# A linear-attention and routed-block kernel on one core: output projections and units moved among the head steps, some rotation sums given to GpSimd, two more banks at the start

## The chip, the cores and the metric

The kernel runs on one core of one Trainium2 chip. The time is device microseconds of one execution. The engines are TensorE (PE), VectorE (DVE), ScalarE (ACT), GpSimd (POOL) and SyncE (SP), which issues nearly all transfers. Each engine runs its own list of instructions in order and waits on semaphores.

## What is computed

```python
xn = layernorm(x)                                   # x: 2048 x 512, fp32
out = x + attn(xn) + ffn(xn)

def attn(x):                                        # 16 heads of width 32, blocks with decay
    q, k, v, u = split(x @ W_qkvu.T)
    q, k = silu(q), silu(k)
    o = decayed_linear_attention(q, k, v)           # a state per head is carried over the tokens
    o = o * rsqrt(mean(o * o) + 1e-6)
    return (u * o) @ W_out.T

def ffn(hidden):                                    # 256 of the 2048 tokens, chosen by w_router
    sel = hidden[top_256(hidden @ w_router)]
    h = rms_norm(sel, ln1)
    q, k, v = rope(h @ wq + bq), rope(h @ wk + bk), h @ wv + bv   # 16 heads of 128, 8 of k and v
    x1 = sel + softmax_causal(q @ k.T / sqrt(128)) @ v @ wo
    mlp = silu(rms_norm(x1, ln2) @ w_gate) * (rms_norm(x1, ln2) @ w_up) @ w_down
    return hidden with the rows of sel replaced by g * (x1 + mlp) + (1 - g) * sel   # g = sigmoid(score)
```

## The kernel before

Nearly every fp32 matmul is made of three in the type fp32r: an operand is split into a rounded high part (made by ACT) and the remainder, the low part (made by DVE or GpSimd), and PE adds high x high, high x low and low x high in one bank (`split_matmuls`, L1177).

**Start.** SP loads s_head, s_hid, x(0), x(1) and the four quarters of K's weights (L383 to L388). ACT makes decay tables from s_head (`decay_tables`, L516), then the highs of the weights and of xT. DVE norms the first two tiles (`ln_stats`, `ln_norm`, L705 and L712), with the power on GpSimd for both at once (`ln_rstd`, L1083), and makes the lows. PE keeps busy with matmuls that nobody reads (`awake`, L1390), turns the tiles (`transposed`, L1184) and projects. A tile of the projections (`project`, L1199) fills one of the banks 2 and 3 in turn and waits until ACT has evacuated the tile before the last (`evacuate`, L484).

**Chunks.** The slots N = -2 to 15 work on chunks of 128 tokens. Slots 0 to 15 make the chunk's scores (L1231), its keys turned (L1263), its attention (L1270) and new state. Between these pieces each slot has four positions (`in_position`): up to slot 13 they project the next tokens; in slots 14 and 15 they hold the first eight `units` of the routed block (L163), each one 128 x 512 piece of its k, v or q projections. A slot's layer norms for later tiles are on DVE (L952 to L959), ahead of and behind `key_decayed` (L808), which makes kdec and frees the bank `turn_bank` for the next transposes.

**Rotation.** A unit of q or k is rotated by DVE in `stage` (L871): six operations read the bank into rope1 and rope2 (L884 to L889), which frees the bank (`unit_b`), and a seventh adds both (L892, `rope_ok`). There is one pair rope1 and rope2, so the next rotation waits for the sum. A unit of v is evacuated by ACT.

**Head steps.** Then come STEPS = 20 steps h, one for each of the 16 heads and four to drain. Step h has on PE the scores of head h (L1442), a unit if `unit_of_step` names one, the transposes of head h - 2's probabilities (L1453), an output projection (`project_out`, L1255) of one 128-token chunk if `out_steps` has h, head h - 3's PV (L1463) and head h - 4's share of the product with wo. Units and output projections take banks 2 and 3 in turn; the order is `bank_jobs` (L173), and a job waits until the one before the last has been read (`bank_free`, L1340): by `stage` or ACT for a unit, by `final` (L910) on DVE for an output projection. An output projection N needs uo(N), loaded by SP into UR (`load_uo`, L351), split by ACT (`split_uo`, L551) and DVE (`uo_low`, L901), and `final` needs `base(N)` of ACT (L620) and the power over the mean squares, which GpSimd makes once for all (`out_rms`, L1089). DVE's order in a step is: SM (L994), `uo_low`, the reciprocal, `stage`, `final`, OTl (L1017). ACT's is: `split_uo`, the exponentials (L648), PT, PN, `base`, `block_hi`, OTh (L668).

**Weights.** The routed block's weights come in 24 blocks of 1 MB (`order`, L155): SP loads a block when GpSimd has made the low of three blocks before (`load_block`, L373), ACT makes the high (`block_hi`, L530), and GpSimd the low in four operations of 128 x 512 (`block_lo`, L1125). `hi_after` and `load_at` (L208, L209) say in which step. After the head steps PE has the last output projections (L1478 to L1481) and the gate, up and down products, one behind the other.

```python
unit_of_step = {0: 8, 1: 9, 2: 10, 3: 11, 4: 12, 5: 13, 7: 14, 8: 15}   # L166
out_steps = [1, 2, 3, 4, 5, 6, 7, 9, 10, 11, 12, 13, 14]                 # L170
```

## Time and profile before

| what | value |
|---|---|
| median of 3 runs | 499.38 us (499.29 to 499.8) |
| the profiled execution | 498.31 us |
| its span, first to last instruction | 496.6 us |
| mean granted clock of TensorE in it | 0.988 |
| busy: PE, DVE, ACT, POOL | 96%, 59%, 47%, 37% |
| matmuls | 4887 |

The profile is one execution. In its rows L is the line of the kernel. A row of the timeline is: start us, us, engine, line, operation, out<-in, shapes, how many are merged (x), and in brackets how long the engine had been idle and what released it. SPq is SP's queue of transfers. `issue` means that nothing the profile shows was waited for. PEclk is the share of TensorE's full clock that was granted. The ends of matmuls are modelled: a matmul's row is longer than the distance to the next one's start.

### The profile page before, as it was taken

What the parts mean: (1) busy time and instruction counts of PE and PEld (TensorE: products, weight loads), DVE (VectorE), ACT (ScalarE), POOL (GpSimd) and SP (SyncE); (2) the same over time, 40 slices, a digit from 0 to 9 for tenths busy, and PEclk for the clock granted to TensorE, in tenths of its full rate; (3) what the DMA queues carried; (4) which work ended last, traced back from release to release, by engine and by line L of the source; (5) the groups of instructions that cost most, each with busy time, mean ns of one, the idle gap of its engine ahead of it and who ended that gap; (6) DMA issues with size and microseconds to landing.
All of it is one profiled execution on the core that took longest, in us unless ns stands there. A gap on an engine that the chain in (4) does not pass through costs nothing.

```text
span 496.6 us, 12003 instructions
## 1 busy us (share of the span) xinstructions
PE 474.7 (96%) x4887; PEld 431.5 (87%) x4887; DVE 294.4 (59%) x631; ACT 232.4 (47%) x420; POOL 183.7 (37%) x173
## 2 busy tenths in 40 slices
PE   7999999999999999999999997999999979999994
PEld 6888899898998989989998786998988758999993
DVE  5889665864388888744447869776753526131221
ACT  8822232221267678221432455667485755454420
POOL 3002241111110222023176857441280440788862
PEclk9999999999999999999999998999999989999998
DMA  7925244212310111005534533555436532454503
GB/s 237 388 85 159 68 129 128 85 35 76 130 44 23 27 44 45 1 23 171 191 107 171 192 112 122 192 213 197 164 147 215 179 118 86 143 176 170 169 1 42
DMA packets 32886, 62.15 MB, mean 125 GB/s; under 512 B 3440, under 2 KB 3456, under 8 KB 32704
## 3 DMA queue, kind: packets, MB, share of 16 engines
q1 hardware_dynamic: 32288, 60.08, 35.8%
q0 software_dynamic: 544, 1.31, 1.4%
q8 instruction: 39, 0.64, 0.5%
q14 instruction: 15, 0.12, 0.1%
HBM read 48.27 MB, written 13.12 MB: 124 GB/s over the span
## 4 chain that ended last, share of the span: by engine, by line
PE 74%; DVE 8%; issue 4%; DMA 4%; ACT 3%; POOL 0%; SPq 0%; DVEq 0%; ACTq 0%; POOLq 0%
PE bank L1226 24%; PE bank L1180 9%; PE bank L1181 9%; PE bank L1182 9%; PE bank L1217 8%; DMA UR<-uo_all 4%; PE bank L1283 3%; PE bank L1246 3%; DVE rope L887 2%; PE bank L1278 2%; DVE A L805 1%; PE bank L1196 1%; PE bank L1267 1%; DVE rope L884 1%; PE bank L1463 1%
## 5 line engine op out<-in xcount | busy, mean ns | idle before, releaser
L1129 POOL TENSOR_TENSOR wlo<-raw,whi 128x512 fp32r<-128x512 f32 x96 | 126.5, 1350 | 92.9 <-ACT whi L533 92.9
L1180 PE MATMUL bank<-HTh,whi 128*128 128x256 f32 x224 | 65.7, 293 | 5.0 <-DVE rope L887 5.0
L1181 PE MATMUL bank<-HTl,whi 128*128 128x256 f32 x224 | 64.0, 286 | 0.0
L1182 PE MATMUL bank<-HTh,wlo 128*128 128x256 f32 x224 | 64.0, 286 | 0.0
L805 DVE TENSOR_TENSOR A<-bank,DEC 128x512 f32<-128x512 f32 x64 | 39.7, 682 | 33.0 <-PE bank L1246 32.4
L1113 POOL TENSOR_TENSOR state_dec<-state,small 128x128 f32<-128x128 f32 x16 | 8.9, 556 | 117.5 <-DVE state L816 117.5
L533 ACT ACTIVATE whi<-raw 128x2048 fp32r<-128x2048 f32 x24 | 45.8, 1906 | 11.5 <-PE bank L1182 11.5
L1180 PEld LDWEIGHTS bank<-HTh,whi 128*128 128x128 f32 x224 | 43.6, 195 | 6.3 <-issue 5.8
L1181 PEld LDWEIGHTS bank<-HTl,whi 128*128 128x128 f32 x224 | 43.6, 195 | 0.3
L1182 PEld LDWEIGHTS bank<-HTh,wlo 128*128 128x128 f32 x224 | 43.6, 195 | 0.0
L1226 PE MATMUL bank<-xTh,WQh 128*128 128x256 f32 x128 | 37.6, 294 | 1.0 <-ACT KT L503 1.0
L1226 PE MATMUL bank<-xTh,WKh 128*128 128x256 f32 x128 | 37.6, 294 | 0.3 <-DVE xTl L738 0.3
L1226 PE MATMUL bank<-xTh,WUh 128*128 128x256 f32 x128 | 37.5, 293 | 0.0
L1226 PE MATMUL bank<-xTh,WKl 128*128 128x256 f32 x128 | 36.2, 283 | 0.0
L1226 PE MATMUL bank<-xTl,WKh 128*128 128x256 f32 x128 | 36.2, 282 | 0.0
L1226 PE MATMUL bank<-xTl,WUh 128*128 128x256 f32 x128 | 36.2, 282 | 0.0
L1226 PE MATMUL bank<-xTl,WQh 128*128 128x256 f32 x128 | 36.1, 282 | 0.0
L1226 PE MATMUL bank<-xTh,WQl 128*128 128x256 f32 x128 | 36.1, 282 | 0.0
L1226 PE MATMUL bank<-xTh,WUl 128*128 128x256 f32 x128 | 36.1, 282 | 0.0
L509 ACT ACTIVATE marks<-marks 128x2048 bf16<-128x2048 bf16 x16 | 30.6, 1911 | 7.4 <-DVE marks L764 7.4
L1040 DVE TENSOR_TENSOR staged<-sg,bank 128x512 f32<-128x512 f32 x8 | 5.5, 688 | 44.2 <-PE bank L1182 44.2
L1087 POOL TENSOR_TENSOR small<-small 128x2 f32<-128x2 f32 (+1 forms) x9 | 6.4, 706 | 65.0 <-issue 41.4
(233 smaller groups left out, 1303.7 us busy)
## 6 DMA issues: line engine op xcount, KB each, us to landing
X<-in_x SPq DMA_DIRECT2D x16, 256.0 KB, 4.7
xn_all<-XN SPq DMA_DIRECT2D x16, 256.0 KB, 2.7
uo_all<-uo SPq DMA_DIRECT2D x16, 256.0 KB, 2.7
raw<-in_wq SPq DMA_DIRECT2D x4, 1024.0 KB, 5.2
UR<-uo_all SPq DMA_DIRECT2D x16, 256.0 KB, 5.4
XR<-in_x SPq DMA_DIRECT2D x16, 256.0 KB, 3.1
raw<-in_wo SPq DMA_DIRECT2D x4, 1024.0 KB, 5.6
out<-XR SPq DMA_DIRECT2D x16, 256.0 KB, 2.4
```

Of the source, the lines that this page charges most:

```text
L509: S.activation(marks[n % 2][:], marks[n % 2][:], ACT.Copy, accum_out=n_ge[:, n:n + 1])\
L533: S.activation(halves(b)[0][:], raw[b % 3][:], ACT.Copy).then_inc(fw_hi, 1)
L805: V.tensor_tensor(A[:, heads, :], tiles4(score_banks[r][:]), DEC[:, heads, :], ALU.mult)\
L887: ins = V.scalar_tensor_tensor(out=rope2[a:a + half, i, :], in0=src[b:b + half], scalar=bias[b:b + half], in1=CS[b:b + half, 1, :], op0=AL ...
L1129: ins = Q.tensor_tensor(low[:, k, :], raw[b % 3][:, k, :], high[:, k, :].bitcast(f32), ALU.subtract)
L1180: T.matmul(dst, lh, rh, start=first, stop=False)
L1181: T.matmul(dst, lh, rl, start=False, stop=False)
L1182: return T.matmul(dst, ll, rh, start=False, stop=last)
L1217: ins = T.matmul(bank[:], xt[:, g % 2, k, j * P:(j + 1) * P], w[:, k, :], start=step == 0, stop=step == steps - 1)
L1226: ins = T.matmul(bank[:, half * GROUP:(half + 1) * GROUP], w[:, k, cols], xt[:, g % 2, k, :], start=m % steps == 0, stop=m % steps == step ...
L1246: ins = T.matmul(score_banks[r][:, j * P:(j + 1) * P], chunk(KT, N)[rows, j, :], chunk(QT, N)[rows, j, :], start=True, stop=True)
L1283: ins = T.matmul(sum_of(h // 4)[c:c + DH], VT[N // CH % 2][:, N % CH, DH * h:DH * h + DH], A[:, by_row(h), :], start=False, stop=True, ski ...
```

## The change

- SP loads x(0) before s_head, and x(1) before s_hid.
- The projections' tiles 2 and 3 go to banks 0 and 1 (`proj_bank`); tiles 2 to 5 wait accordingly.
- `ln_rstd` is done singly for the first two tiles. DVE makes the lows of K in the order 0, both xT, 1, 2, 3. The stats and norm of tile 4 move from slot -2 to before the table DEC, between router(0) and router(1).
- In slot 14 `key_decayed` stands behind the first unit's rotation instead of ahead of it.
- The seventh operation of the rotations of the first eight units (four of them are rotated) moves from DVE to GpSimd (`rotated`), between GpSimd's lows.
- Output projections start in step 0, units 8 to 15 are one step later, with steps 6 and 9 for units alone and 7 for an output projection alone. `split_uo(0)` and `uo_low(0)` move into slot 15, the last chunk's sum of squares to step 0 behind SM, its mean square and its rms matmul to step 1. `split_uo(14)` and `uo_low(14)` move from step 15 to step 17.
- `out_rms` is done in two halves, at slot 9 and in step 2, and `final` waits for its half.

```diff
--- before.py
+++ after.py
@@ -163,11 +163,11 @@
         units = [("K0", 0), ("V0", 0), ("K0", 1), ("V0", 1), ("Q0", 0), ("V1", 0), ("Q0", 1), ("V1", 1)]
         units += [(k, p) for k in ("Q1", "K1", "Q2", "Q3") for p in range(2)]
         in_chunks = 8
-        unit_of_step = {0: 8, 1: 9, 2: 10, 3: 11, 4: 12, 5: 13, 7: 14, 8: 15}
+        unit_of_step = {1: 8, 2: 9, 3: 10, 4: 11, 5: 12, 6: 13, 8: 14, 9: 15}
         PT_AT, PV_AT, WO_AT = 2, 3, 4
         STEPS = FH + WO_AT
         late_outs = (13, 14, 15)
-        out_steps = [1, 2, 3, 4, 5, 6, 7, 9, 10, 11, 12, 13, 14]
+        out_steps = [0, 1, 2, 3, 4, 5, 7, 8, 10, 11, 12, 13, 14]
         out_at = {h: n for n, h in enumerate(out_steps)}
 
         bank_jobs = [("unit", u) for u in range(in_chunks)]
@@ -240,6 +240,10 @@
         def xt_bank(M):
 
             return B[6] if M == 1 else turn_bank
+
+        def proj_bank(tile):
+
+            return B[tile - 2] if tile in (2, 3) else B[2 + tile % 2]
 
         def tiles4(ap):
             return ap.rearrange("p (k m) -> p k m", k=4)
@@ -380,10 +384,10 @@
                     sp.wait_ge(fw_lo, b - 2)
                 sp.dma_start(raw[b % 3][:], source[k[0]](int(k[1]))).then_inc(raw_in[b % 3], 16)
 
+            load_x(0)
             sp.dma_start(shead, s_head.partition_broadcast(P)).then_inc(shead_in, 16)
+            load_x(1)
             sp.dma_start(shid, s_hid).then_inc(shid_in, 16)
-            load_x(0)
-            load_x(1)
             for k in range(NK):
                 sp.dma_start(raw_w["K"][:, k, :], WT_v[:, k, DM:2 * DM]).then_inc(w_raw_k[k], 16)
             load_x(2)
@@ -500,7 +504,7 @@
                     dst = VT[g % 2][:, j, :]
                 else:
                     dst = {"K": KT, "Q": QT, "U": UT}[name][g % 2][:, 2 * j:2 * j + 2, :].rearrange("p k m -> p (k m)")
-                S.activation(dst, B[2 + tile % 2][:], ACT.Silu if name in "KQ" else ACT.Copy).then_inc(proj_sb, 1)
+                S.activation(dst, proj_bank(tile)[:], ACT.Silu if name in "KQ" else ACT.Copy).then_inc(proj_sb, 1)
 
             def count_marks(n):
 
@@ -589,6 +593,8 @@
                     block_hi(1)
                 if N == N_TILES - 2:
                     block_hi(3)
+                if N == N_TILES - 1:
+                    split_uo(0)
                 if N + XT_AHEAD < N_TILES:
                     xt_high(N + XT_AHEAD)
                 count_marks(ranked(N, 1))
@@ -634,11 +640,9 @@
 
             for h in range(STEPS):
                 p, g = h - PT_AT, h - PV_AT
-                if h == 0:
-                    split_uo(0)
                 if h in out_at:
                     split_uo(out_at[h] + 1)
-                if h == out_steps[-1] + 1:
+                if h == FH + 1:
                     split_uo(late_outs[1])
                 if h < FH:
                     act.wait_ge(sm_ok, h + 1)
@@ -648,7 +652,7 @@
                         ins = S.activation(PR[:, h % 2, cols], SM[:, h % 2, cols], ACT.Exp, scale=-1.0,
                                            bias=ntop[:, h % 2, t:t + 1], accum_out=psum_[:, h % 2, t:t + 1])
                     ins.then_inc(exp_ok, 1)
-                if h == 0:
+                if h == 1:
                     mean_square(N_TILES - 1)
                 if 0 <= p < FH:
                     act.wait_ge(pt_ps, p + 1)
@@ -888,8 +892,9 @@
                                                      scalar=bias[b:b + half], in1=CS[b:b + half, 1, :], op0=ALU.add,
                                                      op1=ALU.mult)
                 ins.then_inc(unit_b, 1)
-                dve.wait_ge(unit_b, n + 1)
-                V.tensor_tensor(unit_dst(u), rope1[:], rope2[:], ALU.add).then_inc(rope_ok, 1)
+                if u >= in_chunks:
+                    dve.wait_ge(unit_b, n + 1)
+                    V.tensor_tensor(unit_dst(u), rope1[:], rope2[:], ALU.add).then_inc(rope_ok, 1)
 
             def in_position(N, position):
 
@@ -909,7 +914,8 @@
 
             def final(N):
 
-                dve.wait_ge(out_ps, N + 1), dve.wait_ge(base_ok, N + 1), dve.wait_ge(r_ok, 1)
+                dve.wait_ge(out_ps, N + 1), dve.wait_ge(base_ok, N + 1)
+                dve.wait_ge(r_ok, 1 + N // (N_TILES // 2))
                 V.scalar_tensor_tensor(out=XR[N % NXR][:], in0=job_bank("out", N)[:], scalar=r_all[:, N:N + 1],
                                        in1=XR[N % NXR][:], op0=ALU.mult, op1=ALU.add).then_inc(final_ok, 1)
 
@@ -921,10 +927,10 @@
                 ln_stats(M)
             for M in range(CH):
                 ln_norm(M)
-            first_weights_lo("K", k_w_hi, k_w_lo, (0, 1))
+            first_weights_lo("K", k_w_hi, k_w_lo, (0,))
             for M in range(CH):
                 xt_low(M)
-            first_weights_lo("K", k_w_hi, k_w_lo, (2, 3))
+            first_weights_lo("K", k_w_hi, k_w_lo, (1, 2, 3))
             for M in range(CH, NXN):
                 ln_stats(M)
             first_weights_lo("Q", q_w_hi, q_w_lo)
@@ -933,7 +939,10 @@
             first_weights_lo("V", v_w_hi, v_w_lo)
             xt_low(CH)
             first_weights_lo("U", u_w_hi, u_w_lo)
-            for M in range(NXN):
+            ln_stats(NXN)
+            router(0)
+            ln_norm(NXN)
+            for M in range(1, NXN + 1):
                 router(M)
             dve.wait_ge(decays_ok, 4), dve.wait_ge(masks_ok, 2)
             V.tensor_tensor(DEC[:], DEC[:], tri[:].unsqueeze(1).to_broadcast([P, NH, P]), ALU.mult).then_inc(dec_ok, 1)
@@ -949,12 +958,14 @@
                 if N == HIDDEN:
                     dve.wait_ge(picked, 16 * 2 * NS)
                     normed(0, xsn)
-                for M in ln_tiles(N):
+                for M in ln_tiles(N) if N > -CH else []:
                     ln_stats(M)
-                if 0 <= N < N_TILES - 1:
+                if 0 <= N < N_TILES - 2:
                     key_decayed(N)
                 in_position(N, 0)
-                for M in ln_tiles(N):
+                if N == N_TILES - 2:
+                    key_decayed(N)
+                for M in ln_tiles(N) if N > -CH else []:
                     ln_norm(M)
                     router(M)
                 if N == RANK - 1:
@@ -963,6 +974,8 @@
                 if N == INDEX:
                     token_indices()
                 in_position(N, 1)
+                if N == N_TILES - 1:
+                    uo_low(0)
                 if CH + 1 < N + XT_AHEAD < N_TILES:
                     xt_low(N + XT_AHEAD)
                 if N == CHOOSE:
@@ -981,7 +994,6 @@
                 if N == HIDDEN + 1:
                     selected_scores()
                 in_position(N, 3)
-            squares_summed(N_TILES - 1)
 
             dve.wait_ge(causal_ok, 3)
             for h in range(STEPS):
@@ -996,10 +1008,10 @@
                                                      op1=ALU.min, accum_out=ntop[:, h % 2, t:t + 1])
                     ins.then_inc(sm_ok, 1)
                 if h == 0:
-                    uo_low(0)
+                    squares_summed(N_TILES - 1)
                 if h in out_at:
                     uo_low(out_at[h] + 1)
-                if h == out_steps[-1] + 1:
+                if h == FH + 1:
                     uo_low(late_outs[1])
                 if h < FH:
                     dve.wait_ge(exp_ok, h + 1)
@@ -1086,10 +1098,11 @@
                 s = slice(tiles[0], tiles[-1] + 1)
                 Q.tensor_tensor(rstd[:, s], var_eps[:, s], minus_half[:, s], ALU.pow).then_inc(rstd_ok, len(tiles))
 
-            def out_rms():
-
-                pool.wait_ge(ms_ok, N_TILES)
-                Q.tensor_tensor(r_all, ms_all, minus_half, ALU.pow).then_inc(r_ok, 1)
+            def out_rms(part):
+
+                pool.wait_ge(ms_ok, (part + 1) * N_TILES // 2)
+                some = slice(part * N_TILES // 2, (part + 1) * N_TILES // 2)
+                Q.tensor_tensor(r_all[:, some], ms_all[:, some], minus_half[:, some], ALU.pow).then_inc(r_ok, 1)
 
             def rows_rms(n):
 
@@ -1122,6 +1135,11 @@
                                              in_offset=bass.IndirectOffsetOnAxis(ap=idx[:, t:t + 1], axis=0))\
                             .then_inc(picked, 16)
 
+            def rotated(u):
+
+                pool.wait_ge(unit_b, kq_count(u))
+                Q.tensor_tensor(unit_dst(u), rope1[:], rope2[:], ALU.add).then_inc(rope_ok, 1)
+
             def block_lo(b):
                 pool.wait_ge(fw_hi, b + 1)
                 high, low = halves(b)
@@ -1129,7 +1147,8 @@
                     ins = Q.tensor_tensor(low[:, k, :], raw[b % 3][:, k, :], high[:, k, :].bitcast(f32), ALU.subtract)
                 ins.then_inc(fw_lo, 1)
 
-            ln_rstd(range(CH))
+            for M in range(CH):
+                ln_rstd([M])
             Q.memset(state[:], 0.0).then_inc(state_zero, 1)
             ln_rstd(range(CH, NXN))
             for N in slots_of_chunks:
@@ -1141,11 +1160,24 @@
                     rows_rms(0)
                 if N == INDEX:
                     gather()
-                if N >= N_TILES - 3:
-                    block_lo(2 * (N - (N_TILES - 3)))
-                    block_lo(2 * (N - (N_TILES - 3)) + 1)
+                if N == N_TILES // 2 + 1:
+                    out_rms(0)
+                if N == N_TILES - 3:
+                    block_lo(0)
+                    block_lo(1)
+                if N == N_TILES - 2:
+                    block_lo(2)
+                    rotated(0)
+                    block_lo(3)
                 if -1 <= N < N_TILES - 1:
                     state_decayed(N + 1)
+                if N == N_TILES - 2:
+                    rotated(2)
+                if N == N_TILES - 1:
+                    block_lo(4)
+                    rotated(4)
+                    rotated(6)
+                    block_lo(5)
                 if N == 1:
                     out_weights_lo()
                 if N == 0:
@@ -1155,10 +1187,11 @@
                         Q.affine_select(out=causal[:, blk * P:(blk + 1) * P], in_=causal[:, blk * P:(blk + 1) * P],
                                         compare_op=ALU.is_ge, fill=-1.0e38, base=0, pattern=[[-1, P]],
                                         channel_multiplier=1).then_inc(causal_ok, 1)
-            out_rms()
             for h in range(STEPS):
                 if h in hi_after:
                     block_lo(block_of[hi_after[h]])
+                if h == 2:
+                    out_rms(1)
             rows_rms(1)
             for b in range(block_of["G1"], len(order)):
                 block_lo(b)
@@ -1206,9 +1239,9 @@
                     pe.wait_ge(xt_lo, CH * (g + 1))
                 if g == 0 and j == 0 and name in "VU":
                     pe.wait_ge(v_w_lo if name == "V" else u_w_lo, NK)
-                if tile >= 2:
-                    pe.wait_ge(proj_sb, tile - 1)
-                bank = B[2 + tile % 2]
+                if tile >= 4:
+                    pe.wait_ge(proj_sb, tile - 3 if tile < 6 else tile - 1)
+                bank = proj_bank(tile)
                 steps = 3 * NK
                 for step in range(steps):
                     if name == "V":
@@ -1444,7 +1477,7 @@
                     ins.then_inc(sc_ps, 1)
                 if h in unit_of_step:
                     unit(unit_of_step[h])
-                if h == 0:
+                if h == 1:
                     rms(N_TILES - 1)
                 p = h - PT_AT
                 if 0 <= p < FH:
```

## Rows read from the trace of the kernel before

**Rows 1.** The page's table of engines: busy us (share of the span) xinstructions, per engine.

```profile
PE 474.7 (96%) x4887; PEld 431.5 (87%) x4887; DVE 294.4 (59%) x631; ACT 232.4 (47%) x420; POOL 183.7 (37%) x173
```

**Rows 2.** Table of stages: window, its us, busy us (x) per engine, PEclk, DMA.

```profile
46.00:260.00 214.00, 213.98 (x3049) 197.74 (x3048) 137.01 (x288) 85.96 (x145) 48.25 (x51) 1.00 0.24 79
260.00:300.00 40.00, 37.92 (x439) 33.86 (x438) 30.09 (x60) 17.27 (x26) 28.59 (x22) 1.00 0.50 168
```

**Rows 3.** Waits of PE: released by; us in total, times, longest us.

```profile
PE bank L1180 <- DVE rope L887: 5.0, 4, 2.9
...
PE bank L1463 <- DVE OTl L1017: 2.3, 3, 1.1
...
PE bank L1226 <- ACT KT L503: 1.0, 1, 1.0
PE bank L1196 <- DVE kdec L811: 0.9, 1, 0.9
```

**Rows 4.** Table of stages, PE alone: window, us, busy us (x), PEclk, DMA.

```profile
16.00:18.00 2.00, 1.20 (x10) 1.00 1.05 386
...
308.00:313.00 5.00, 5.00 (x31) 0.71 0.62 212
...
404.00:407.00 3.00, 3.00 (x12) 0.59 0.01 3
```

**Rows 5.** Timeline of the start, all engines.

```profile
0.79 0.39 SPq L383 DMA_DIRECT2D small<-in_s_head  x1
...
1.71 0.90 SPq L334 DMA_DIRECT2D X<-in_x  x2
...
7.60 1.00 DVE L718 TENSOR_SCALAR XN<-X,small 128x512 f32<-128x512 f32 x2 [0.90 <-POOL small L1087]
...
8.96 1.09 ACT L481 ACTIVATE xTh<-bank 128x512 fp32r<-128x512 f32 x2
...
10.92 1.28 DVE L750 TENSOR_TENSOR WKl<-raw_K,WKh 128x512 fp32r<-128x512 f32 x2
```

**Rows 6.** Timeline of DVE around the first chunk.

```profile
32.65 0.55 DVE L718 TENSOR_SCALAR XN<-X,small 128x512 f32<-128x512 f32 x1 [0.67 <-POOL small L1087]
...
44.58 0.69 DVE L811 TENSOR_TENSOR kdec<-bank,KD 128x512 f32<-128x512 f32 x1
```

**Rows 7.** Timeline of N = 14 and 15: PE, DVE and GpSimd.

```profile
269.64 0.36 PE L1180 MATMUL bank<-HTh,whi 128*128 128x256 f32 x1 [0.89 <-DVE rope L887]
...
279.08 2.47 DVE L805 TENSOR_TENSOR A<-bank,DEC 128x512 f32<-128x512 f32 x4
...
280.64 1.30 POOL L1108 TENSOR_TENSOR qdec<-QT,QD 128x512 f32<-128x512 f32 x1
281.90 5.48 POOL L1129 TENSOR_TENSOR wlo<-raw,whi 128x512 fp32r<-128x512 f32 x4
...
285.56 0.36 PE L1180 MATMUL bank<-HTh,whi 128*128 128x256 f32 x1 [0.93 <-DVE rope L887]
```

**Rows 8.** The chain that ended last: start us, us, what; one projection's half.

```profile
50.82 3.06 PE bank L1226 x24
```

**Rows 9.** Timeline of steps 0 and 1: DVE and ACT.

```profile
296.57 0.69 DVE L869 TENSOR_TENSOR uol<-UR,uoh 128x512 fp32r<-128x512 f32 x1
...
298.62 1.90 ACT L533 ACTIVATE whi<-raw 128x2048 fp32r<-128x2048 f32 x1
...
300.90 1.72 DVE L892 TENSOR_TENSOR QR<-rope,rope 128x512 f32<-128x512 f32 x1
...
303.09 1.23 DVE L869 TENSOR_TENSOR uol<-UR,uoh 128x512 fp32r<-128x512 f32 x1
```

**Rows 10.** Timeline of steps 14 to 16: SP, ACT and PE.

```profile
393.45 0.45 SPq L357 DMA_DIRECT2D UR<-uo_all  x1
...
399.24 0.63 ACT L557 ACTIVATE uoh<-UR 128x512 fp32r<-128x512 f32 x1 [3.11 <-DMA UR<-uo_all]
...
401.22 0.52 PE L1453 MATMUL bank<-ident,PN 128*128 128x128 f32 x3 [1.80 <-issue]
```

## The prediction

> **What bounds the kernel now.** I read the engine table first: PE is busy for 96% of the span and no other engine for more than 59% [rows 1]. So PE's instructions set the end, and only time in which PE stands still or runs at its lower clock can be won. The change removes no matmul. The table of stages says where such time lies: from 46 to 260 us PE is busy for 213.98 of 214.00, with nothing to win [rows 2]. The table of waits then names the stops: 5.0 us in four of them until a rotation's read of its bank (L887) is over, 2.3 us in three until OTl is there (L1017), and single ones of 1.0 (evacuation of KT) and 0.9 (kdec) [rows 3]; one of 1.80 stands before the transposes at L1453 [rows 10]. The granted clock adds the other half: it is 0.71 in 308 to 313, behind the longest stop, and 0.59 in 404 to 407, behind the two stops after 399 [rows 4]. At 1.2 GHz against 2.4 these two cost 5 x 0.29 = 1.45 and 3 x 0.41 = 1.2 us. All this together is about 14 us, of which the change aims at four parts.
>
> **Part 1, the start and the first chunk.** The first two tiles are normed one by one, x(0) is loaded ahead of s_head, tiles 2 and 3 of the projections get banks 0 and 1, and the lows of K are made in the order 0, xT, xT, 1, 2, 3. x(0) is issued at 0.79 instead of 1.71, 0.9 us earlier, and DVE's 0.90 us wait for the pair's power becomes shorter [rows 5]. But the xT evacuations stand behind ACT's decay tables, which start on s_head, and that is issued 0.45 later than before. So ACT's chain (tables, two highs of K, then xTh at 8.96) slips to about 9.3 [rows 5], and I take nothing for the earlier norm. The lows 1 to 3 of K now follow xTl; each is some 0.65 us [rows 5], while PE needs the next after three matmuls, 0.36 us. PE's first tile so loses about 0.75 us. Against that, tile 2 no longer waits 1.0 for KT [rows 3], nor tile 4 for QT: PE is some tenths ahead at 25 us. How much does not matter, for PE's next stop, at 45.4, is for kdec, the last of DVE's unbroken queue [rows 3, 6]. That queue starts about 0.4 us earlier, as it waits for the third tile's transposes, and it loses 0.67 us waiting for the power of tile 4, most of which router(0) now covers [rows 6]; I take 0.5. **Term: -0.9**, bounds 0 (DVE's queue does not move) and -1.9 (the whole stop goes as well).
>
> **Part 2, the rotations of the chunks on GpSimd.** At N = 14 kdec (0.61 from start to start) moves behind the first rotation, so the bank is read 0.6 earlier and the stop of 0.89 [rows 7] becomes 0.3. At N = 15 the rotation's sum leaves DVE, but DVE then waits for the scores of PE, which end at 278.7: mask(15) starts at 278.8 instead of 279.08, and the stop of 0.93 becomes 0.65 [rows 7]. The stop before the first unit of the head steps is what is left of the 5.0, about 0.2 [rows 3, 7], and stays: it hangs on the rotation of unit 6, which starts when gated(15) has ended. The sums themselves cost 4 x 1.3 us of GpSimd, by the row of qdec, the same form [rows 7], and GpSimd is busy for 28.59 of 40 us there [rows 2]. They are hidden if each ends before the next rotation on DVE: rotated(2) stands behind block_lo(3) and state_decayed and ends at about 282.0, where DVE asks at 282.2; rotated(4) stands behind q_decayed and the 5.48 us of block_lo(4) and ends at 290.2 (all in old time), where DVE asks at 291.0 [rows 7]. These margins of 0.2 and 0.8 are thin; a miss costs its own length at once. Behind rotated(6) block_lo(5) is queued, which ends 5 us later than now, at 301; its readers are units of step 3, after 309, and one load (below). out_rms(0) is put at N = 9, where GpSimd has time, and nothing waits for it there. **Term: -0.9**, bounds +1.0 (both margins missed by some 0.9) and -1.8.
>
> The Trainium skill (GPSIMD Engine Reference, opening text) calls GpSimd the wrong choice for ordinary elementwise work, with VectorE about twice as fast. The trace agrees: 1.30 on GpSimd against 0.69 on DVE for the same width [rows 7, 9]. By the rule alone the sums would cost 0.6 us each, 2.4 in all; in the sum above they cost nothing, since DVE has left them and GpSimd's turn is not waited for.
>
> **Part 3, steps 0 to 3.** Now PE stops 2.9 us before unit 10 and then runs at the lower clock for a while [rows 3, 4]. In old time the new order runs like this. out(0) starts at 294.1 on unit 6's bank. DVE goes from the rotation of unit 6 straight to SM(0), without the sum. final(0), new in step 0, waits for base(0) on ACT, which comes after the table load, uoh, the exponentials and PN: 298.8. Behind base(0) stands block_hi (1.90), then uoh(2) and exp(1) [rows 9], so DVE reaches the rotation of unit 8 at 302.5 and ends it at 305.5. PE has out(0), scores, unit 8, out(1) and scores behind it at 303.9 (24 matmuls of a unit take 3.06, as those of a projection do [rows 8]; an out has 12 of double width, and I take 2.85) and waits 1.7 us. SP is the next one late: load_block(8) waits for block 5's lows (301), and load_uo(3) is queued behind it, so it is issued at 301.5 and, with the 5.8 us that the load of uo(14) took [rows 10], lands at 307.3. ACT's exp(2) and DVE's rotation of unit 9 wait behind it: another stop of 0.6 before unit 10. From step 3 on a full step has 6.4 us of DVE against 8.6 of PE and no stop is left, as now. Instead of 2.9 + 1.45 us, and some 0.4 that the pieces around them lose, there are 2.3. **Term: -2.5**. The clock is the open size: the stop of 1.0 before 18.2 drew no lower clock, that of 2.9 did [rows 3, 4], and 1.7 lies between them. If it falls, 1.4 comes back. Bounds -0.5 and -4.0.
>
> What the two-input operations of DVE lose beside GpSimd is in this path: uol took 0.69 and, with GpSimd busy, 1.23, the sum of unit 8 1.72 [rows 9]. I have put in 0.5 for one. The Trainium skill (SBUF — State Buffer, "Who interferes with whom") says that such an operation and a GpSimd instruction that reads SBUF exclude each other for the whole instruction. By that rule uol(1) and uol(2) could lose up to 1.3 each, and this term would be -0.5; I weigh it as a rival.
>
> **Part 4, the end of the head steps.** split_uo(14) now stands in step 15, and ACT waits 3.11 us in it for a load issued at 393.45, with exp(15), the copy of PT and OTh behind it [rows 10]. It moves to step 17, where the load has long landed. exp(15) then starts when SM(15) is there, at 397.6, some 2.1 earlier, and everything after it moves with it. PE's stops of 1.80 and, before the PV matmuls, 1.1 [rows 3, 10] become 0 and 0.9; then the clock stays up (1.2). **Term: -3.2**, bounds -1.5 (clock falls all the same, block_hi in step 16 takes the place) and -4.0 (the first of the three stops for OTl goes too, since one out fewer stands in the run of bare out steps).
>
> The matmuls from 418 on follow each other without a stop and depend on loads started by PE's own progress, so nothing is given back there. **Sum: -0.9 - 0.9 - 2.5 - 3.2 = -7.5 us.** The profiled execution took 498.31 us (span 496.6); it would take 490.8. The median of the runs is 1.07 higher, 499.38, so I predict 491.9.
>
> **Rivals.**
> 1. The forecast, 489.5 to 494: 0.50.
> 2. Lock and clock: uol stretched as in the 1.72 row and a lower clock behind the new stops in step 2 and step 16, 1.4 + 1.2 less: -5, 494.4. For it: stops remain at exactly these two places. Against it: each is shorter than those that drew the clock down. 0.22.
> 3. More than I count: final(0) early enough, no stop before unit 9, kdec's stop gone: -10.5, 488.9. For it: DVE and ACT are idle for a third of the time there. 0.14.
> 4. Nothing: K's lows and block 5's lows are late, and what the new order wins at 304 it loses at once in steps 1 to 3. 499.4. Against it: part 4 does not hang on that. 0.06.
> 5. Slower: the GpSimd queue. Rotations stand behind four subtractions of 1.3 to 1.7 us; block 5's lows gate load_block(8), load_uo(3) and, through ACT's order, every exponential. Each us by which they come later than 304 stops PE for a us, and at half clock for longer. It decides from about 311 on (a delay of 10 us, against 5 counted); then steps 2 to 4 lose 8 to 10 and the end is 501.5. GpSimd's free 11 us in 260 to 300 [rows 2] speak against it. 0.08.
>
> **How the numbers follow.** About 0.2% (1 us) is what a measurement of this kernel can tell from no change. Cases 1 to 3 are faster, 0.86; case 4 the same, 0.06; case 5 slower, 0.08. The range runs from case 3's side, 488.3, to the upper side of case 2, 495.8, and leaves out cases 4 and 5 and the far edges.
>
> **What would show it.** Right: no waits of PE for KT and QT; kdec's wait 0.7 or less; stops for L887 of about 0.3, 0.65, 0.2, 1.7 and 0.6, the longest before unit 9; clock near 1.00 in the old 400 to 410; ACT's uoh(14) without a wait. Wrong: PE waiting in the first K tile for more than 1 us, stops on GpSimd's rope sums, a clock under 0.8 behind step 2, or UR loads that stop ACT in every step.

## The result, and the profile after

| | before | changed kernel |
|---|---|---|
| median | 499.59 us (499.29 to 500.45, 4 runs) | 491.69 us (491.37 to 492.96, 4 runs) |
| ratio, with its 95% interval | 1 | 0.9844 [0.9822, 0.9866] |
| profiled execution, its span | 498.31 us, 496.6 us | 491.94 us, 490.2 us |
| mean granted clock | 0.988 | 0.996 |

The kernel is 7.9 us faster by the medians. The forecast was 491.9, range 488.3 to 495.8. The two profiled executions differ by only 6.4 us (the one of before lies 1.3 under its median here, the changed kernel's 0.25 over its own), and the working below is against that figure.

The table of engines of the changed kernel:

```profile
PE 473.1 (97%) x4887; PEld 429.7 (88%) x4887; DVE 291.4 (59%) x627; ACT 231.9 (47%) x420; POOL 189.6 (39%) x179
```

The matmuls are as many as in [rows 1]. GpSimd has 6 us more, DVE 3 less. What changed is where PE stands still. The waits of PE, released by whom, us in total, times, longest:

```profile
PE bank L1213 <- DVE rope L891: 3.4, 6, 1.5
...
PE bank L1229 <- DVE kdec L815: 1.3, 1, 1.3
PE bank L1496 <- DVE OTl L1029: 1.1, 2, 0.9
PE bank L1259 <- DVE xTl L742: 1.0, 1, 1.0
PE bank L1316 <- issue: 0.9, 3, 0.3
```

Against [rows 3]: the rotation's 5.0 is now 3.4 and its longest stop is 1.5 instead of 2.9, OTl's 2.3 is 1.1, and the wait for KT is gone. kdec's has grown from 0.9 to 1.3, the one for xTl ahead of the first K tile from 0.3 to 1.0, and the last row is new. The same stops one by one, in PE's timeline (start us, us, instruction, in brackets the idle time before it and its releaser):

```profile
44.72 0.63 PE L1229 MATMUL bank<-ident,XA 128*128 128x128 f32 x4 [1.27 <-DVE kdec L815]
...
270.23 0.35 PE L1213 MATMUL bank<-HTh,whi 128*128 128x256 f32 x1 [0.26 <-DVE rope L891]
...
285.87 0.36 PE L1213 MATMUL bank<-HTh,whi 128*128 128x256 f32 x1 [0.65 <-DVE rope L891]
...
294.44 0.47 PE L1213 MATMUL bank<-Woh,uoh 128*128 128x512 f32 x1 [0.26 <-DVE rope L891]
...
306.03 0.35 PE L1213 MATMUL bank<-HTh,whi 128*128 128x256 f32 x1 [1.48 <-DVE rope L891]
...
313.24 0.36 PE L1213 MATMUL bank<-HTh,whi 128*128 128x256 f32 x1 [0.35 <-DVE rope L891]
...
321.11 0.35 PE L1213 MATMUL bank<-HTh,whi 128*128 128x256 f32 x1 [0.37 <-DVE rope L891]
...
397.77 0.67 PE L1496 MATMUL bank<-PT,VA 128*128 128x256 f32 x2 [0.91 <-DVE OTl L1029]
```

No stop stands before the transposes of head 14 any more, where [rows 10] had 1.80. The clock, from the table of stages (window, its us, busy us of PE, PEld, DVE, ACT, POOL with counts, PEclk, DMA):

```profile
308.00:313.00 5.00, 4.89 (x29) 3.97 (x27) 4.29 (x13) 4.08 (x9) 0.00 (x0) 1.00 0.82 249
...
404.00:407.00 3.00, 3.00 (x14) 2.40 (x13) 1.22 (x3) 0.00 (x0) 0.84 (x1) 1.00 0.23 62
```

It is 1.00, the upper level (2.4 GHz), in both windows where [rows 4] had 0.71 and 0.59. A stop of 1.5 us in step 2 and two of 0.2 and 0.9 at 394 and 398 did not bring it down.

Where the time went follows from the lead of the changed kernel over the one before at the same instruction of PE:

| at | before | changed | lead | since the row above |
|---|---|---|---|---|
| scores of chunk 1 | 53.80 | 53.11 | 0.69 | 0.69 |
| PV of chunk 11 begins | 224.04 | 223.38 | 0.66 | 0 |
| scores of chunk 12 | 229.01 | 230.24 | -1.23 | **-1.9** |
| PV of chunk 15 | 288.60 | 288.91 | -0.31 | 0.92 |
| scores of step 10 | 365.69 | 364.06 | 1.63 | 1.94 |
| transposes behind the head steps | 417.78 | 411.33 | 6.45 | 4.82 |

The third row is the surprise. PE's timeline in the changed kernel there:

```profile
223.97 0.83 PE L1316 MATMUL bank<-A,VT 128*32 128x128 f32 x16
225.10 0.43 PE L1316 MATMUL bank<-A,VT 128*32 128x128 f32 x5 [0.30 <-issue]
225.82 0.44 PE L1316 MATMUL bank<-A,VT 128*32 128x128 f32 x5 [0.29 <-issue]
226.55 0.39 PE L1316 MATMUL bank<-A,VT 128*32 128x128 f32 x4 [0.30 <-issue]
```

Behind the first 16, the PV matmuls of chunk 11 come in groups of about five with 0.3 us between them, and nothing that the profile shows is waited for. With the slower groups it costs 1.9 us. The stage from 224 to 228 us of the changed kernel:

```profile
224.00:228.00 4.00, 3.11 (x77) 2.26 (x71) 0.95 (x3) 0.26 (x2) 1.52 (x2) 1.00 0.48 135
```

and of the kernel before:

```profile
224.00:228.00 4.00, 4.00 (x114) 3.72 (x114) 0.95 (x3) 1.26 (x3) 3.06 (x4) 1.00 0.61 176
```

PE issued 77 matmuls instead of 114, at a granted clock of 1.00 in both.

### The profile page after: what moved, and what is told of

It is laid out like the page before. It is cut to its first block and busy times, and to the rows that moved or that the text cites. A ratio compares the mean times of both kernels' runs of the same rounds, so it can differ in the third digit from the quotient of the medians.

```text
span 490.2 us, 12005 instructions
## 1 busy us (share of the span) xinstructions
PE 473.1 (97%) x4887; PEld 429.7 (88%) x4887; DVE 291.4 (59%) x627; ACT 231.9 (47%) x420; POOL 189.6 (39%) x179
## 5 line engine op out<-in xcount | busy, mean ns | idle before, releaser
L1099 POOL TENSOR_TENSOR small<-small 128x2 f32<-128x2 f32 (+1 forms) x10 | 7.4, 743 | 63.6 <-issue 37.2
```

Of the source, the lines that this page charges most:

```text
L1099: Q.tensor_tensor(rstd[:, s], var_eps[:, s], minus_half[:, s], ALU.pow).then_inc(rstd_ok, len(tiles))
```

## The experiments

Twelve kernels ran, in three groups. The kernels of one group ran on one chip, another for each group, and share the runs of before: median 499.12 (11 runs) in the first group, 498.29 (11) in the second, 498.05 (23) in the third. Ratios are to those.

### First group: the changed kernel with one part put back

**The changed kernel again.** No edit.

> The changed kernel itself, as the measure for the three beside it. In its first profile PE stood still for 1.9 us between 224 and 227 in the middle of the matmuls of L1316, with no semaphore named, which the profile before does not have. Theory (chance of an execution, the supply of PE's instructions): this profile need not show it, and then the span is about 1.9 us shorter, near 488.3. Rival (it belongs to the new program, whose instructions lie elsewhere): it stands at the same place again. Time about 491.7.

Measured: 492.68 us, 0.9874 [0.9854, 0.9894], span 490.0. The stops are the same to 0.03 us (kdec 1.3, longest rotation 1.5, 0.9 in three inside L1316), but for the one before unit 11, which is 0.64 instead of 0.37, and the one for xTl, 1.2 instead of 1.0. Stops and clock of this kernel repeat to some 0.3 us, and the medians of two sets of runs are 1 us apart, so single medians settle no part under 1 us.

**Part 4 undone.**

```diff
-                if h == FH + 1:
+                if h == out_steps[-1] + 1:
                     split_uo(late_outs[1])
...
-                if h == FH + 1:
+                if h == out_steps[-1] + 1:
                     uo_low(late_outs[1])
```

> The changed kernel with split_uo(14) and uo_low(14) back in step 15. Theory (part 4 of the prediction): ACT waits some 3 us in step 15 for UR, exp(15) starts 2 us later, PE stops about 1.8 and 1.1 us in step 16 and the clock falls; 3.2 us slower than the changed kernel, 494.9. Rival (the end was won by the shorter run of bare out steps and the earlier loads, the place of the split does nothing): within 0.5 us of the changed kernel.

Measured: 496.23 us, 0.9926 [0.9902, 0.9949], 3.5 us slower than the changed kernel beside it. Its PE and ACT timelines have the stops of [rows 10] again:

```profile
396.95 0.67 PE L1496 MATMUL bank<-PT,VA 128*128 128x256 f32 x2 [0.20 <-DVE OTl L1029]
400.95 0.52 PE L1486 MATMUL bank<-ident,PN 128*128 128x128 f32 x3 [1.71 <-issue]
402.56 1.19 PE L1496 MATMUL bank<-PT,VA 128*128 128x256 f32 x2 [1.09 <-DVE OTl L1029]
...
398.97 0.63 ACT L561 ACTIVATE uoh<-UR 128x512 fp32r<-128x512 f32 x1 [3.03 <-DMA UR<-uo_all]
```

ACT waits 3.0 us for the load, PE 1.7 for ACT, and the granted clock over 404 to 407 is 0.72.

**The order of units and outs undone**, the rest of the change kept.

```diff
-        unit_of_step = {1: 8, 2: 9, 3: 10, 4: 11, 5: 12, 6: 13, 8: 14, 9: 15}
+        unit_of_step = {0: 8, 1: 9, 2: 10, 3: 11, 4: 12, 5: 13, 7: 14, 8: 15}
-        out_steps = [0, 1, 2, 3, 4, 5, 7, 8, 10, 11, 12, 13, 14]
+        out_steps = [1, 2, 3, 4, 5, 6, 7, 9, 10, 11, 12, 13, 14]
```

> The changed kernel with the old tables of steps: units from step 0, out projections from step 1, step 6 with an out alone and step 8 with a unit alone. Theory (part 3): a stop of 2.5 us or more before unit 10 with the lower clock behind it comes back in place of 1.5 + 0.4 + 0.4, and a stop for OTl in steps 13 to 15; 1.9 us for the first and about 1 us for the second, 494.6. Rival (the sums on GpSimd have already relieved DVE in steps 0 to 3, the order of units and outs is worth nothing): within 0.7 us of the changed kernel.

Measured: 492.94 us, 0.9882 [0.9862, 0.9901], span 490.3 against 490.0. PE's waits:

```profile
PE bank L1213 <- DVE rope L891: 2.7, 4, 1.5
...
PE bank L1496 <- DVE OTl L1029: 2.1, 3, 0.9
```

With the old order the longest stop, now before unit 10, is also 1.5 and no other follows it. The new order, which stands first in the change's name, is worth nothing that can be measured. Something else in the change shortened the stop of 2.9.

**The sums of the chunks' rotations back on DVE.**

```diff
-                if u >= in_chunks:
-                    dve.wait_ge(unit_b, n + 1)
-                    V.tensor_tensor(unit_dst(u), rope1[:], rope2[:], ALU.add).then_inc(rope_ok, 1)
+                dve.wait_ge(unit_b, n + 1)
+                V.tensor_tensor(unit_dst(u), rope1[:], rope2[:], ALU.add).then_inc(rope_ok, 1)
...
-                    rotated(0)
...
-                    rotated(2)
...
-                    rotated(4)
-                    rotated(6)
```

> The changed kernel with the four rotation sums back on DVE (kdec of slot 14 stays behind the rotation). Theory: 0.3 us more before unit 6, and in step 0 the sum of unit 6 delays uol(1), PN(0), base(0), block_hi and with them the rotation of unit 8 by about 1.0 us; 493.0, and 494.4 if the longer stop draws the clock down. Rival (GpSimd's queue is the later one, since block 5's lows and through them load_block(8) and load_uo(3) come 5 us later than before because of the sums): the stops before units 10 and 11 go, and the time is 0.5 us lower than the changed kernel's or the same.

Measured: 491.83 us, 0.9860 [0.9838, 0.9882], span 489.8. From the PE timeline:

```profile
286.21 0.35 PE L1207 MATMUL bank<-HTh,whi 128*128 128x256 f32 x1 [0.94 <-DVE rope L891]
...
306.32 0.35 PE L1207 MATMUL bank<-HTh,whi 128*128 128x256 f32 x1 [1.46 <-DVE rope L891]
```

The stop in slot 15 is 0.3 longer without GpSimd's sums, as the working said. The two stops of 0.35 and 0.37 at 313 and 321 are gone, as the rival said, but not for its reason. Block 5's lows do end earlier (296.9 instead of 301.1), yet block 8's load is issued at 301.25 instead of 301.16: in SP's queue it stands behind the store of out(0), which waits for `final(0)`. At unit 10 PE comes 0.3 later and only uses up the stop that was there. At unit 11 ACT's split starts at 315.41 instead of 315.88, when its load has landed, though that load was issued 0.3 later, and the uol behind it takes 0.73 instead of 1.47, while GpSimd makes lows beside both. In the repeat above this same stop was 0.3 longer. So the sums win 0.3 in slot 15, PE loses that again at unit 10, and that they cost anything at unit 11 is not shown.

### Second group

**The change's start undone**, all else kept: the load order, the banks of tiles 2 and 3, the order of K's lows, the paired norms and the place of tile 4's norm.

```diff
-            load_x(0)
             sp.dma_start(shead, s_head.partition_broadcast(P)).then_inc(shead_in, 16)
-            load_x(1)
             sp.dma_start(shid, s_hid).then_inc(shid_in, 16)
+            load_x(0)
+            load_x(1)
...
-            return B[tile - 2] if tile in (2, 3) else B[2 + tile % 2]
+            return B[2 + tile % 2]
...
-            for M in range(CH):
-                ln_rstd([M])
+            ln_rstd(range(CH))
```

> The changed kernel with the whole start put back (order of the first loads, banks of tiles 2 and 3, single powers, order of K's lows, norm of tile 4). Theory (part 1): the first chunk comes 0.7 us later, kdec's stop is 0.9, tile 2 waits 1.0 again; by itself 0.7 us slower than the changed kernel, 492.9. Second theory: the stall of 1.9 us at L1316 near 225 us belongs to where the instructions of PE lie, which the start's waits shift; if it goes here, the time is 1.2 us lower instead, 491. Rival for the stall (it belongs to the chip or to the collision with the gather, which stands at the same place in PE's work in both): it stays.

Measured: 491.06 us, 0.9864 [0.9838, 0.9891], span 488.4. PE is 0.1 us ahead of the kernel before through all the chunks instead of 0.67. The gaps in the PV matmuls of chunk 11 are not there (114 matmuls in 224 to 228, busy 4.00). Both theories seemed to hold, the second by the vanished gaps; the third group took that reading back.

**Part 4 alone**, on the kernel before (the two lines of part 4 above).

> The kernel before with only split_uo(14) and uo_low(14) moved from step 15 to step 17. Theory (part 4 holds by itself): ACT's wait of 3.1 us in step 15 goes, the stops of 1.80 and 1.1 us of PE become 0 and 0.9 and the clock stays up; 3.4 us faster than the kernel before in the profile. Rival (only together with the new order of steps): less than 1 us faster. The stall of 1.9 us at L1316 around 225 us should be absent, as PE's list is that of the kernel before.

Measured: 494.84 us, 0.9941 [0.9920, 0.9961], span 492.7, so 3.4 us by the medians and 3.9 by the spans. Its waits of PE:

```profile
PE bank L1180 <- DVE rope L887: 5.0, 4, 2.9
...
PE bank L1463 <- DVE OTl L1017: 2.0, 3, 0.9
```

and its stages, with columns as above:

```profile
300.00:320.00 20.00, 17.08 (x100) 15.29 (x99) 17.08 (x42) 11.15 (x27) 10.43 (x8) 0.91 0.46 156
395.00:425.00 30.00, 28.35 (x165) 24.25 (x164) 12.95 (x29) 18.01 (x32) 11.24 (x9) 1.00 0.36 114
```

The same two stages of the kernel before:

```profile
300.00:320.00 20.00, 17.09 (x100) 15.31 (x99) 17.15 (x42) 11.14 (x27) 10.45 (x8) 0.91 0.46 159
395.00:425.00 30.00, 26.39 (x134) 21.66 (x133) 12.64 (x29) 16.73 (x31) 8.76 (x8) 0.94 0.34 112
```

Steps 0 to 3 are untouched, and at the end the clock goes from 0.94 over 30 us to 1.00. In stretches of 5 us it was 0.80 and 0.86 over 400 to 410, which is 1.7 us. With the stops (1.8 + 2.3 before, 2.0 now, 2.1 less) that is 3.8 of the 3.9.

**Eight tiny matmuls more at PE's start**, in the changed kernel, to shift PE's instructions against the pieces in which they are fetched.

```diff
+            for n in range(8):
+                pe.wait_ge(masks_ok, 1)
+                T.matmul(B[0][:, 0:1], ident[:], ident[:, 0:1], start=True, stop=True)
             awake(12)
```

> The changed kernel with eight additional matmuls of one column at the very start of PE's list, ahead of the ones that nobody reads; they cost nothing there, since PE waits for the first tile. Theory (the stall of 1.9 us at L1316 near 225 us hangs on how PE's instructions fall into the pieces in which they are fetched): the stall goes or moves to another place, and the time falls by up to 1.9 us. Rival (it hangs on the data and the transfers of that stretch): it stays at the same matmuls, time as the changed kernel.

Measured: 492.20 us, 0.9880 [0.9854, 0.9907], span 491.0. The gaps in chunk 11 are gone (131 matmuls in 224 to 230, busy 6.00), but the start is later: the extra matmuls, 16 in the trace, hold PE from 2.50 to 5.94, and the first K tile begins at 13.89 instead of 11.40. So they did not cost nothing, as was expected, and the time says little. Taken alone the vanished gaps looked like the answer. The third group took it back.

**Two repairs together**, in the changed kernel: kdec(0) ahead of slot 0's norms, and Q2's highs and lows one step later, with the loads that stand behind them.

```diff
+                if N == 0:
+                    key_decayed(0)
                 for M in ln_tiles(N) if N > -CH else []:
                     ln_stats(M)
-                if 0 <= N < N_TILES - 2:
+                if 0 < N < N_TILES - 2:
                     key_decayed(N)
...
-        hi_after = {0: "Q2", 2: "O0", 4: "Q3", 6: "O1", 8: "O2", 9: "O3", 12: "G0", 16: "U0"}
-        load_at = {0: "Q3", 1: "O1", 3: "O2", 5: "O3", 7: "G0", 9: "U0", 10: "G1", 13: "U1", 17: "D0"}
+        hi_after = {1: "Q2", 2: "O0", 4: "Q3", 6: "O1", 8: "O2", 9: "O3", 12: "G0", 16: "U0"}
+        load_at = {1: "Q3", 2: "O1", 3: "O2", 5: "O3", 7: "G0", 9: "U0", 10: "G1", 13: "U1", 17: "D0"}
```

> The changed kernel with two further moves. kdec of chunk 0 is made before the layer norms of slot 0 instead of behind them; block_hi and block_lo of Q2 stand in step 1 instead of 0, and the loads of Q3 and O1 one step later, behind load_uo(3) and load_uo(4). Theory (what stops PE in steps 0 to 3 is ACT's block_hi ahead of exp(1), and SP's load_block(8) ahead of load_uo(3)): the stop of 1.5 before unit 9 shrinks to about 0.3, the two of 0.4 go, and the stop of 1.3 for kdec goes; 3.2 us faster than the changed kernel, 488.8. Rival (DVE is the bound there: its own work between the rotation of unit 6 and that of unit 8 fills the time): the stop before unit 9 stays at 1 us or more and only kdec's 1.3 is won.

Measured: 488.26 us, 0.9812 [0.9788, 0.9836], span 487.7. The stop before unit 9 is 0.28 instead of 1.48. The stop for kdec is gone, but a new one stands some 6 us behind it, for the low of xT that now comes later; its row among PE's waits:

```profile
PE bank L1328 <- DVE xTl L742: 1.4, 1, 1.4
```

So the repair in the chunks only moved the stop: DVE does the same norms ahead of that low. The repair in the head steps is the one that pays. This kernel has no gaps in chunk 11 either, so its ratio against the changed kernel's holds some 1.9 us that the edits did not win.

### Third group

**Q2 one step later, alone** (the second half of the diff above).

> The changed kernel with Q2's highs and lows one head step later, and block 3's and 4's loads with them; nothing else. Theory (the load of UR that stands behind the load of block 8 made the stop before unit 9): that stop falls from 1.5 to 0.3, and the kernel is 1.2 us faster than the changed one, about 0.982 of the kernel before, if the stops of 0.3 us inside the PV matmuls of chunk 11 stay as in the changed kernel. Rival (the gain of the kernel with both edits was the vanished stops of chunk 11, which went away with the moved kdec(0)): this one is as fast as the changed kernel, 0.985 to 0.987.

Measured: 488.74 us, 0.9819 [0.9791, 0.9847], span 486.4, the shortest of all. PE's timeline at units 9 and 10, then ACT's wait for a load of UR there:

```profile
303.05 0.36 PE L1213 MATMUL bank<-HTh,whi 128*128 128x256 f32 x1 [0.30 <-DVE rope L891]
...
310.22 0.36 PE L1213 MATMUL bank<-HTh,whi 128*128 128x256 f32 x1 [0.31 <-DVE rope L891]
```

```profile
312.23 0.63 ACT L561 ACTIVATE uoh<-UR 128x512 fp32r<-128x512 f32 x1 [1.76 <-DMA UR<-uo_all]
```

The long stop is gone and none replaces it: ACT still waits 1.8 us for a load, but PE does not stop for what follows. The number is the theory's, the cause is not. In the changed kernel the load behind block 8's lands at 307.19, when the stop before unit 9 is already over (306.03). What made it was ACT's order: Q2's high stood ahead of uo(2)'s split, and DVE's low of uo(2) and the rotation of unit 8 waited for that. First the changed kernel, then this one:

```profile
299.00 1.90 ACT L537 ACTIVATE whi<-raw 128x2048 fp32r<-128x2048 f32 x1
300.81 0.61 ACT L561 ACTIVATE uoh<-UR 128x512 fp32r<-128x512 f32 x1
...
302.93 0.46 DVE L888 SCALAR_TENSOR_TENSOR rope<-bank,bqkv,CS 128x256 f32<-128x256 f32 x1
```

```profile
297.21 0.62 ACT L561 ACTIVATE uoh<-UR 128x512 fp32r<-128x512 f32 x1
...
299.93 0.48 DVE L888 SCALAR_TENSOR_TENSOR rope<-bank,bqkv,CS 128x256 f32<-128x256 f32 x1
```

The rotation starts 3.0 us earlier, where PE is 1.8 ahead; the difference is the 1.2 of the stop.

And chunk 11 has no gaps (101 matmuls in 224 to 228, busy 4.00). Of the 3.8 us by which this span is shorter than the changed kernel's, 1.9 appear in chunk 11, 1.2 at unit 9, and 0.7 at unit 11. So the ratio cannot tell the theory from the rival, which gave the whole gain to the gaps; the trace can, and each has about half. Up to the head steps PE's instructions are those of the changed kernel, one for one. So the gaps do not hang on how they fall into fetched pieces, and what the eight extra matmuls seemed to show need not be their doing.

**The start undone and Q2 later.** The two diffs together.

> The kernel with the start put back, and Q2 one step later. The start put back alone was at 0.9864 and had no stop in chunk 11. Theory (gains of separate places add up): stop before unit 9 of 0.3 instead of 1.5, 1.2 us less, 0.984, span about 487.2. Rival (what is won before unit 9 is lost at units 10 to 13, whose weights now come one step later): 0.986.

Measured: 489.06 us, 0.9823 [0.9798, 0.9848], span 487.5. The long stop is gone here too. The kernel with the start undone and Q2 in its old place had no gaps either, 0.9864 and a span of 488.4, so the later Q2 is worth 0.9 us by the spans of two kernels without gaps, and 2.0 by the ratios, whose intervals overlap. Against the kernel above, on the same chip, the start is worth 0.3 us by the medians, less than they can tell.

**The start alone**, on the kernel before (the diff of the second group's first kernel, the other way round).

> The kernel before with the change's start alone: single norms, x(0) first, two more banks, K's lows in the new order. Theory: the stop for kdec at 45 us is earlier, and PE leads by 0.7 us from there on as in the changed kernel. That is all if PE has no gaps in its PV matmuls, so 498.6 where before is 499.3 (0.9985). Rival (the 1.9 us lost in chunk 11 belong to this part of the change whatever else is in the program): PE shows the gaps of 0.3 us there, and the kernel is 1.2 us slower than before, 1.0025.

Measured: 497.00 us, 0.9982 [0.9963, 1.0001]. The interval just holds 1. No gaps in chunk 11, so the rival is out. The profiled execution is the longest of its set, 500.48, and its timeline is no measure of the part: PE's clock fell in the first K tile and again at 403.

**uo(0) alone**, on the kernel before: its split and low in slot 15, tile 15's squares behind SM(0).

```diff
+                if N == N_TILES - 1:
+                    split_uo(0)
                 if N + XT_AHEAD < N_TILES:
                     xt_high(N + XT_AHEAD)
...
-                if h == 0:
-                    split_uo(0)
...
+                if N == N_TILES - 1:
+                    uo_low(0)
...
-            squares_summed(N_TILES - 1)
...
                 if h == 0:
-                    uo_low(0)
+                    squares_summed(N_TILES - 1)
```

> The kernel before with uo(0)'s split moved to the last slot of the chunks and the squares of tile 15 behind the first scores; the order of units and outs as before, the sums on DVE. Theory (this move, not the new order, shortened the stop of 2.9 us): that stop is 1.5 and the clock behind it stays at 1.00, so 1.4 + 1.4 less, with 0.4 to 1 given back at later stops: 1.9 to 2.5 us faster, 0.995 to 0.996. Rival (it takes the new order or GpSimd's sums as well): stop 2.5 to 2.9, clock 0.7 behind it, 0.9985 to 1.000.

Measured: 495.81 us, 0.9959 [0.9938, 0.9979], 2.2 us less. PE's waits:

```profile
PE bank L1181 <- DVE rope L887: 4.0, 5, 1.5
...
PE bank L1464 <- DVE OTl L1018: 2.2, 3, 1.1
...
PE bank L1454 <- issue: 1.4, 1, 1.4
```

and its longest stop in the timeline:

```profile
305.82 0.36 PE L1181 MATMUL bank<-HTh,whi 128*128 128x256 f32 x1 [1.51 <-DVE rope L887]
```

The stop of 2.9 is 1.5 and the granted clock from 300 to 320 is 1.00 instead of 0.91, with the old order and the sums on DVE. This small move gives what part 3 gave. The rotation of unit 9, which ends the stop, starts at 302.70 instead of 304.41. Of these 1.7 us, 0.7 are there because unit 8's rotation starts sooner, and 1.0 because its sum on DVE takes 0.69 instead of the 1.72 of [rows 9], as GpSimd's operations lie otherwise beside it.

The profiled execution is 4.1 us shorter than the one of before. At the scores of step 10 it leads by 2.3; the other 1.8 come at 400 to 410, where the clock stayed at 1.00. The medians hold only 2.2, and the mean clocks of this set go from 0.989 to 0.998, the profiled one's, so the clock at that place is not the same in every execution.

## Why the prediction was right

By the parts, in us against the profiled execution, and by the experiment that made the part alone or undid it:

| part | forecast | in the trace | by experiment (medians) |
|---|---|---|---|
| 1, start | -0.9 | -0.67 | -0.9 by the ratio (interval -1.8 to 0), -0.3 |
| 2, sums and kdec(14) | -0.9 | -0.92 | the sums alone: 0; kdec(14) was not made alone |
| 3, steps 0 to 3 | -2.5 | -1.94 | uo(0)'s move alone: -2.2; the order alone: 0 |
| 4, end of the head steps | -3.2 | -4.82 | -3.4 alone, -3.5 within the change |
| not foreseen, chunk 11 | 0 | +1.9 | open |
| sum | -7.5 | -6.5 | |

The parts made alone (start, uo(0), part 4) multiply to 0.9982 x 0.9959 x 0.9941 = 0.9882, beside 0.9874 and 0.9844 for the whole: little is left for the order and the sums.

**Part 1** came out for the reason given: PE's next stop decides, and DVE's queue sets it. That queue ended 0.7 us sooner, though kdec's stop is not shorter (0.9 to 1.3), since PE came there 1.04 us earlier. The forecast that a stop of "0.7 or less" would show it was wrong. The reordered lows cost PE what was said: from the first to the last matmul of K's two tiles there are 6.5 us instead of 5.9, against "about 0.75". The stop for xTl ahead of them grew from 0.3 to 1.0. The waits for KT and QT are gone, and 0.35 of what they freed is what PE then stood longer before kdec. This is what the forecast said of it, that it does not matter.

What it did not say is that the start also moved a stop to a place where the clock can fall. In three kernels with the new start, of nine, the stop for xTl was 1.5 to 1.9 us and the granted clock was 0.59 over 13 to 17.2, 1.7 us lost; a fourth with a stop of 1.6 kept 1.00. In the five with the old start that stop was 0.3 and the clock did not fall. Whether the start causes this is not shown.

**Part 2** was right in every row: 0.26 and 0.65 against "0.3" and "0.65", and the third stop of 0.26 where 0.2 was expected. GpSimd kept its thin margins:

```profile
280.78 1.29 POOL L1141 TENSOR_TENSOR KR<-rope,rope 128x512 f32<-128x512 f32 x1
...
283.28 5.48 POOL L1147 TENSOR_TENSOR wlo<-raw,whi 128x512 fp32r<-128x512 f32 x4
288.72 1.28 POOL L1141 TENSOR_TENSOR QR<-rope,rope 128x512 f32<-128x512 f32 x1
```

rotated(2) ends at 282.07, where DVE asks at 282.75; rotated(4) at 290.0, asked at 291.3. But two thirds of the part are carried by the one line that moves kdec(14). The price of the sums was put in another part, as a load behind block 5's later lows that leaves PE a stop of 0.6. The lows did end at 301.1, but with the sums on DVE, where they end at 296.9, the load is issued at the same time (301.25 against 301.16), so that cause was wrong.

**Part 3** has the right rows for the wrong reason. Stops of 1.7 and 0.6 were forecast, 1.48 and 0.35 with another of 0.37 came; the times of the chain behind the second are those described, almost to the tenth. In SP's and ACT's timelines:

```profile
301.16 0.38 SPq L385 DMA_DIRECT2D raw<-in_wq  x1
301.64 0.45 SPq L361 DMA_DIRECT2D UR<-uo_all  x1
...
307.19 0.63 ACT L561 ACTIVATE uoh<-UR 128x512 fp32r<-128x512 f32 x1 [2.63 <-DMA UR<-uo_all]
```

Forecast were 301.5 for the issue and 307.3 for the landing. The issue also follows the end of block 5's lows (301.1), as described, but they delay it by 0.3 us at most: the store of out(0) and a load of x stand ahead of it in SP's queue until 300.8. The step that failed is "in old time the new order runs like this": I gave the whole gain to the new order, and the experiments give it to split_uo(0), uo_low(0) and the squares, which no longer stand in front of step 0's work on ACT and DVE. The old order would have done as well. The clock was the open size, and priced too low: 1.45, where 0.75 and 0.91 over 305 to 315 make 1.7. It stayed at 1.00 behind 1.5 us, so rival 2 is out, though half of its mechanism is there:

```profile
296.23 1.24 DVE L873 TENSOR_TENSOR uol<-UR,uoh 128x512 fp32r<-128x512 f32 x1 [0.24 <-ACT uoh L561]
...
301.45 1.48 DVE L873 TENSOR_TENSOR uol<-UR,uoh 128x512 fp32r<-128x512 f32 x1 [0.97 <-ACT uoh L561]
...
305.92 1.17 DVE L897 TENSOR_TENSOR QR<-rope,rope 128x512 f32<-128x512 f32 x1
...
308.81 0.69 DVE L873 TENSOR_TENSOR uol<-UR,uoh 128x512 fp32r<-128x512 f32 x1
```

All through 295.6 to 306.6 GpSimd makes lows, and DVE's operations with two inputs take 1.17 to 1.48; the first one behind them takes 0.69. The two uols lose 0.55 and 0.79. By the rule of the Trainium skill (SBUF — State Buffer, "Who interferes with whom") such operations exclude a GpSimd instruction that reads SBUF for its whole length; the trace agrees, at under one such instruction (1.37 us) each. What one operation loses hangs on where it falls between GpSimd's: in the 14 traces the uols beside lows took 0.69 to 1.83, one 3.66, and those without lows beside them 0.67 to 0.69. Of the 1.3 us together 0.5 stood in the sum.

**Part 4** had the mechanism and too small a size. The terms named were stops of 1.80 and 1.1 becoming 0 and 0.9, and 1.2 for the clock. Measured on the kernel with part 4 alone: 2.1 of stops and 1.7 of clock. The clock term was taken from a window of 3 us at 0.59, which left out the first microsecond of the lower clock; over 400 to 410 it makes the 1.7. In the full change the stops at OTl shrink as well, from 2.3 in three to 1.1 in two, which was the far bound of the forecast ("the first of the three stops for OTl goes too"): 1.8 + 1.2 + 1.7 = 4.7, beside 4.82 in the trace. With the old order of outs they stay at 2.1 in three. That is the one thing the order does, and what it gives there (1.0) it pays back as the two stops before units 10 and 11 (0.7).

**What was missed.** The text said that from 46 to 260 there was nothing to win, and took the stretch as safe. It cost 1.9 us. Five traces have the gaps: the changed kernel, its repeat and the other three kernels of the first group. The nine others have none: the kernel before and all eight of the second and third group. Two explanations by the edits fall. It is not the new start, since the kernels with it in the third group are clean, one of them with PE's instructions unchanged up to the head steps. It is not the head steps' order or the sums, since two of the five have those undone. Nor is it the gather of the chosen tokens on GpSimd: in all 14 traces its third transfer starts 0.35 us ahead of these matmuls. What all runs allow is that it belongs to the chip or to where the program lies in memory. No kernel was profiled in two of the groups, which would tell, so this stays open. The kernel before was timed in all three, and its median in the first is 0.8 to 1.1 us above the others, which would fit the chip, but no trace of those executions shows chunk 11. In the gap's place the trace shows one 16 KB transfer on the queue of instructions, at 225.1, and the clean kernel with Q2 later has the same one at 225.4.

That the total came out at 491.69 against 491.9 is luck. The profile was to show 490.8 and showed 491.94: part 4 was better by 1.6, chunk 11 worse by 1.9, and parts 1 and 3 together worse by 0.8. To that the forecast added 1.07, by which the profiled execution of before lay under its median, and the changed kernel's lay 0.25 over its own. Without the gaps the forecast would have been some 2 us too slow, still inside its range.

## What to carry over

When a change has several edits near one stop, ask of each alone whether it moves the last releaser of that stop. Here a small split that stood ahead of a stage's first work did all, and the reordering that stands first in the change's name did nothing that could be measured.

Work that nobody waits for yet can still stand ahead of work that somebody waits for. A block's conversion and its loads one step later took a stop of 1.5 us to 0.3, since 1.9 us of ACT no longer stood ahead of a split. The kernels with it are the best of this study, 0.9812 and 0.9819 of the time before, but half of what they gain on the changed kernel is the gaps that they do not have.

An edit that makes a predicted number come true has not shown the predicted cause. Two explanations here fitted the times, block 5's later lows behind the stops at units 10 and 11 and a load behind the stop before unit 9. Both fell when the time of the load was read: 0.1 later instead of earlier in the one, 1.2 behind the stop in the other.

A lower clock is priced over the whole stretch until it reads 1.00 again, not over the window where it is lowest: 1.7 us at both places, where 1.45 and 1.2 had been read.
